# A fourth tile, in SBUF, for the ring of the decays, and the first batch's gate projection placed behind its softplus

## What is computed

```
xc, res = split(x @ W_in.T + b_in)
u       = silu(conv(xc) + conv_b)
dlt, Bm, Cm = split(u @ W_x.T)
delta   = softplus(dlt @ W_dt.T + b_dt)
dA      = exp(delta * A);  dBu = delta * Bm * u
carry   = dA * carry + dBu;  y = sum_n(carry * Cm)
y       = (y * silu(res)) @ W_out.T + b_out
```

## Time and profile before

| | |
|---|---|
| time, median of 3 runs | 2794.74 us (2792.72 to 2795.35) |
| the profiled execution's own time | 2792.28 us |
| its span | 2790.5 us |
| busy: TensorE, VectorE, ScalarE, GpSimd | 87%, 77%, 65%, 74% of the span |
| GpSimd, last product of the mixers | ends at 2207.35 us |
| behind it | the last batches' attention, then the experts; GpSimd is idle there |

### The profile page before, as it was taken

How to read it: one execution, slowest core, us unless ns; L and a number is a source line. 1 busy time by engine, 2 the same in 40 slices (tenths; PEclk the granted TensorE clock), 3 DMA queues, 4 the chain that set the end, 5 groups by cost and what they waited for, 6 DMA issues and landing times. The chain is left out here.

```text
span 2790.5 us, 49779 instructions
## 1 busy us (share of the span) xinstructions
PE 2424.6 (87%) x14816; PEld 1660.6 (60%) x14816; DVE 2140.0 (77%) x3586; ACT 1802.9 (65%) x3972; POOL 2074.5 (74%) x968
## 2 busy tenths in 40 slices
PE   3578888888889898889889888898888879999998
PEld 2345666666666666666666666666665545555554
DVE  1778999999999999999999999999999832322332
ACT  1666777877888888777877787878777541211111
POOL 2999999999999999999999999999999500000000
PEclk8788999999999999999999999999998879999999
DMA  3456566666666666666666666666666360343221
GB/s 118 128 133 149 150 165 168 165 158 157 157 169 166 160 158 165 165 162 168 166 169 164 162 164 166 165 173 163 166 172 158 86 180 12 91 126 96 78 79 31
DMA packets 319323, 399.65 MB, mean 143 GB/s; under 512 B 115697, under 2 KB 256241, under 8 KB 314962
## 3 DMA queue, kind: packets, MB, share of 16 engines
q1 hardware_dynamic: 303698, 384.91, 53.5%
q10 hardware_dynamic: 15360, 11.55, 1.5%
HBM read 300.86 MB, written 94.37 MB: 142 GB/s over the span
## 5 line engine op out<-in xcount | busy, mean ns | idle before, releaser
L506 POOL TENSOR_TENSOR arena<-arena 128x1024 f32<-128x1024 f32 x512 | 1208.2, 2363 | 66.6 <-DMA arena<-w_dram 42.3
L582 ACT ACTIVATE dA_ps<-arena,a_neg 128x252 f32<-128x252 f32 x2048 | 868.7, 461 | 330.4 <-DVE dA_ps L787 172.0
L764 DVE TENSOR_TENSOR_SCAN arena<-dA_ps,arena 128x512 f32<-128x512 f32 x672 | 803.6, 1208 | 112.5 <-ACT dA_ps L582 88.0
L516 POOL TENSOR_TENSOR arena<-arena 128x1024 f32<-128x1024 f32 (+1 forms) x416 | 808.1, 1943 | 17.8 <-DVE arena L764 17.2
L764 DVE TENSOR_TENSOR_SCAN dA_ps<-dA_ps,arena 128x512 f32<-128x512 f32 x352 | 416.2, 1205 | 3.9 <-POOL arena L506 3.7
L887 PE MATMUL a_ps<-xT,w_conv 128*128 128x256 f32 x1536 | 369.8, 391 | 0.0
L829 DVE TENSOR_REDUCE mx<-s_ps 128x2 f32<-128x512 f32 x497 | 334.0, 672 | 23.2 <-PE s_ps L887 23.2
L887 PEld LDWEIGHTS a_ps<-xT,w_conv 128*128 128x128 f32 x1536 | 288.4, 194 | 54.1 <-issue 16.5
L887 PE MATMUL y_ps<-arena,sel 128*32 128x256 f32 x4096 | 257.5, 393 | 55.5 <-DVE m_rows L835 27.8
L640 ACT ACTIVATE probs<-st_ps 128x512 f32<-128x512 f32 x493 | 285.3, 579 | 29.7 <-PE st_ps L887 25.5
L887 PE MATMUL s_ps<-k_st,q_st 96*128 96x256 f32 x994 | 260.6, 344 | 43.7 <-DVE mx L829 28.0
(11 more groups left out here) (111 smaller groups left out, 3272.9 us busy)
## 6 DMA issues: line engine op xcount, KB each, us to landing
arena<-delta_dram SPq DMA_DIRECT2D x512, 128.0 KB, 2.8
arena<-w_dram SPq DMA_DIRECT2D x512, 128.0 KB, 3.2
arena<-bc_dram SPq DMA_DIRECT2D x128, 256.0 KB, 4.5
q_st<-q_parts_dram SPq DMA_DIRECT2D x512, 64.0 KB
k_st<-k_parts_dram SPq DMA_DIRECT2D x512, 64.0 KB
w_dram<-u SPq DMA_DIRECT2D x32, 512.0 KB, 2.8
delta_dram<-delta SPq DMA_DIRECT2D x32, 512.0 KB, 3.8
k_parts_dram<-parts SPq DMA_DIRECT2D x32, 512.0 KB, 4.0
```

The source lines that it names most:

```text
L506: pool.tensor_tensor(dBu[:, n % NB], w_r[:, n // RP % 2, t % RP].unsqueeze(1).to_broadcast([P, QS, L]), bc_r[:, b.par, 0], ALU.mult).then_ ...
L516: pool.tensor_tensor(h[:, n % NH, states], h[:, n % NH, states], bc_r[:, b.par, 1, states], ALU.mult).then_inc(s_hC, 1)
L582: last = nc.scalar.activation(dA[n % NDA][:, q, :, 1:], delta_r[:, n // (2 * RP) % 2, t % RP].rearrange("p (c t) -> p c t", t=CH)[:, :, 1: ...
L764: nc.vector.tensor_tensor_scan(dst, decays, dBu[:, n % NB, 2 * half:2 * half + 2].rearrange("p q t -> p (q t)"), 0.0, ALU.mult, ALU.add).t ...
```

## The change

It has two parts.

**The ring.** `NDA` becomes 4. The fourth member is an SBUF tile `dA_sb` of the same shape; the other three stay in PSUM. Half tile n uses member n modulo 4.

**The start.** SyncE loads the bias parts first, then the convolution's weights and x, then `w_x`, `w_dt` and `w_gate` under a semaphore of their own with no wait between them, then waits for `N_SET` and loads the other seven. VectorE forms the scaled bias rows first; the copy into `bias` becomes a ScalarE instruction; then the convolution's weights. For the first batch alone the four gate projections, their copies and the gate's silu move from the convolutions to behind the softplus (with a table load more). The x projection of the first batch waits for the three front weights, the first state sum for the other seven.

```
-NDA = 3
+NDA = 4
...
-        dA = [bank(f"dA_ps{i}", [P, 2, NCH, CH]) for i in range(NDA)]
+        dA = [bank(f"dA_ps{i}", [P, 2, NCH, CH]) for i in range(NDA - 1)]
+        dA.append(sb("dA_sb", [P, 2, NCH, CH]))
...
+        front_weights = [(w_x[:], "w_x"), (w_dt[:], "w_dt"), (w_gate[:], "w_gate")]
         weights = [
-            (w_gate[:], "w_gate"), (w_x[:], "w_x"), (w_dt[:], "w_dt"), (sel[:], "sel"), (w_out[:], "w_out"),
+            (sel[:], "sel"), (w_out[:], "w_out"),
...
+            for tile, name in bias_parts:
+                sp.dma_start(tile, io[name]).then_inc(s_bias_ld, 16)
             sp.dma_start(w_xc.rearrange("p q t -> p (q t)"), io["w_xc"]).then_inc(s_conv_ld, 16)
             sp.dma_start(conv_rows, io["conv_rows"].partition_broadcast(P)).then_inc(s_conv_ld, 16)
-            for tile, name in bias_parts:
-                sp.dma_start(tile, io[name]).then_inc(s_bias_ld, 16)
             def load_weights():
+                for tile, name in front_weights:
+                    sp.dma_start(tile, io[name]).then_inc(s_front, 16)
+                sp.wait_ge(s_const_v, N_SET)
                 for tile, name in weights:
                     sp.dma_start(tile, io[name]).then_inc(s_const, 16)
-                    sp.wait_ge(s_const_v, N_SET)
                 sp.wait_ge(s_const_p, 4)
...
             act.wait_ge(s_bias_ld, 16 * len(bias_parts))
+            act.wait_ge(s_const_v, N_ROWS)
+            nc.scalar.activation(bias[:], rows, ACT.Copy).then_inc(s_const_a, 1)
             nc.scalar.activation(a_neg[:], a_neg[:], ACT.Exp).then_inc(s_const_a, 1)
...
             def silu(b):
                 act.wait_ge(s_conv, b.value(2, 2))
                 nc.scalar.activation(u[:], u[:], ACT.Silu).then_inc(s_u, 1)
-                act.wait_ge(s_gate, b.value(2, 2))
-                nc.scalar.activation(gate[:, b.par], gate[:, b.par], ACT.Silu).then_inc(s_gsilu, 1)
+                if b.back(1):
+                    silu_gate(b)
                 nc.scalar.preload_act_table_set(EXP_LN)
+            def first_gate(b):
+                if not b.back(1):
+                    for half in range(2):
+                        gate_evac(half)(b)
+                    silu_gate(b)
+                    nc.scalar.preload_act_table_set(EXP_LN)
...
+                (O_SP + 2, first_gate),
...
+            dve.wait_ge(s_bias_ld, 16 * len(bias_parts))
+            nc.vector.tensor_tensor(rows, rows, row_scales, ALU.mult).then_inc(s_const_v, 1)
             dve.wait_ge(s_conv_ld, 32)
...
-            dve.wait_ge(s_bias_ld, 16 * len(bias_parts))
-            nc.vector.tensor_tensor(rows, rows, row_scales, ALU.mult).then_inc(s_const_v, 1)
-            dve.wait_ge(s_const_v, N_CONV - 3)
-            nc.vector.tensor_copy(bias[:], rows).then_inc(s_const_v, 1)
-            dve.wait_ge(s_const_v, N_CONV - 2)
+            dve.wait_ge(s_const_a, 1)
...
-                    if m == 0 and not b.back(1):
-                        pe.wait_ge(s_const, 16 * N_WEIGHTS)
-                        pe.wait_ge(s_const_v, N_SET)
-                        pe.wait_ge(s_const_p, 4)
...
+            def first_gate(b):
+                if not b.back(1):
+                    for m in range(ND):
+                        gate_proj(m)(b)
...
             def x_proj(b):
+                if not b.back(1):
+                    pe.wait_ge(s_front, 16 * len(front_weights))
+                    pe.wait_ge(s_const_v, N_SET)
...
+                    if m == 0 and not b.back(1):
+                        pe.wait_ge(s_const, 16 * N_WEIGHTS)
+                        pe.wait_ge(s_const_p, 4)
...
-                *[(O_GATE + 4 * (m // 2), gate_proj(m)) for m in range(ND)],
+                *[(O_GATE + 4 * (m // 2), later_gate(m)) for m in range(ND)],
+                (O_SP + 1, first_gate),
```

More of the change, by code:

```diff
@@ L279, in mixers @@
         s_const = sem("weights_loaded")
+        s_front = sem("front_weights_loaded")
         s_const_p = sem("const_set_pool")
@@ L329, in mixers @@
         N_WEIGHTS = len(weights)
-        N_CONV = 6 + NDA + TAPS * KD
+        N_ROWS = 3 + NDA
+        N_CONV = 5 + NDA + TAPS * KD
         N_SET = N_CONV + 2
@@ L547, in gate_evac, with silu_gate @@
                 return piece
+            def silu_gate(b):
+                act.wait_ge(s_gate, b.value(2, 2))
+                nc.scalar.activation(gate[:, b.par], gate[:, b.par], ACT.Silu).then_inc(s_gsilu, 1)
             def silu(b):
@@ L551, in silu, with later_gate_evac, piece @@
                 nc.scalar.activation(u[:], u[:], ACT.Silu).then_inc(s_u, 1)
-                act.wait_ge(s_gate, b.value(2, 2))
-                nc.scalar.activation(gate[:, b.par], gate[:, b.par], ACT.Silu).then_inc(s_gsilu, 1)
+                if b.back(1):
+                    silu_gate(b)
                 nc.scalar.preload_act_table_set(EXP_LN)
+            def first_gate(b):
[4 more added lines that the diff above has]
+                    nc.scalar.preload_act_table_set(EXP_LN)
+            def later_gate_evac(half):
+                def piece(b):
+                    if b.back(1):
+                        gate_evac(half)(b)
+                return piece
             def xp_evac(b):
@@ L703, in _ @@
                 (O_SILU, silu),
-                *[(O_GATE + 4 * half + 2, gate_evac(half)) for half in range(2)],
+                *[(O_GATE + 4 * half + 2, later_gate_evac(half)) for half in range(2)],
+                (O_SP + 2, first_gate),
                 (O_K + 1, high(s_k_mm, s_k_hi, s_q_dram, 1)),
@@ L745, in _ @@
             nc.vector.memset(xp[RANK + 2 * NS:RANK + 2 * NS + 1], 1.0).then_inc(s_const_v, 1)
-            dve.wait_ge(s_const_a, 1)
+            dve.wait_ge(s_const_a, 2)
             nc.vector.tensor_scalar(a_neg[:], a_neg[:], -1.0, None, ALU.mult).then_inc(s_const_v, 1)
@@ L918, in gate_proj, with later_gate, piece @@
                 return piece
+            def first_gate(b):
+                if not b.back(1):
+                    for m in range(ND):
+                        gate_proj(m)(b)
+            def later_gate(m):
+                def piece(b):
+                    if b.back(1):
+                        gate_proj(m)(b)
+                return piece
             def x_proj(b):
+                if not b.back(1):
+                    pe.wait_ge(s_front, 16 * len(front_weights))
+                    pe.wait_ge(s_const_v, N_SET)
                 pe.wait_ge(s_u, b.value(1, 1))
```

## The result

The changed kernel took 3040.39 us in the median (3035.71 to 3043.85, 4 runs) against 2795.05 us for the kernel before on the same chip: ratio 1.0876, 95% interval 1.0857 to 1.0895. Forecast were 3150 us. The direction came out as forecast, and so did the lock between the two engines; the size was 245 us instead of 355.

The account below looks back on a forecast made before the run. GpSimd was taken to set the pace, at 64.2 of 66.7 us a batch. 2792.3 + 374 (GpSimd held) - 16 (start) - 0 (fourth bank) = 3150 us; stated range 2765 to 3260, the forecast's own 3060 to 3260.

Parts of the forecast that it names:

- The mechanism: On the SBUF tile, VectorE instructions with two SBUF inputs and GpSimd products reading SBUF block each other; forecast's chance 0.54.
- the 768-column product: At the start, a VectorE product with both inputs in SBUF ran 0.95 us under GpSimd's memset, not held.
- upper end: In each batch, GpSimd is held for 8 scans and 3 products on the SBUF tile: 11.7 us a batch.
- nearer to the copy: Two-SBUF-input cases likened to the start's 2.40 us VectorE copy, which ended 0.41 us behind GpSimd's memset.
- GpSimd stands still for the whole of each: GpSimd loses the full length of 8 scans (1.208 us) and 3 products (0.676) a batch, 374 us in 32 batches.
- 3060: Lower edge of the forecast's own range: the lock lasts three quarters of the VectorE instruction.
- VectorE's waits: Each of 11 VectorE instructions on the tile waits some 1.0 us for GpSimd: 11 us a batch, taken as hidden.
- GpSimd stays the bound: In the batch loop, VectorE at 72.6 us stays below GpSimd's new period of 78.4, so VectorE's waits are hidden.
- rival 3: VectorE becomes the bound: each of 11 instructions waits a whole 2.36 us, 87.6 us a batch, 3445 us; chance 0.08.
- What the fourth place buys: ScalarE runs one half tile further ahead: 0 to 0.7 us a batch, taken as 0.2, then 0 in the sum.
- ScalarE's writes to SBUF: 16 exponentials a batch write SBUF instead of PSUM: 0 to 0.125 us more each, within ScalarE's 13 us of room.
- The start: First batch: convolutions follow each other, gates move behind the softplus; GpSimd's first product near 54.5 instead of 70.65, -16 us.

## Why the prediction was right, and where its sizes were off

- **The mechanism** was right: a VectorE instruction with two SBUF inputs and a GpSimd product shut each other out, in both directions, the second standing still until the first is done. The run with memsets shows it, and shows that the memset beside which the 768-column product ran freely was no proof of the contrary. It also takes away the reason that the prediction gave from the rows for its upper end, that the case is "nearer to the copy": the copy has one input and stood beside a memset, which reads nothing, and beside memsets the scans were free. So that copy is another case than the scans, and by the rows alone the choice was luck.
- **"GpSimd stands still for the whole of each", 11.7 us a batch, 374 us**, is the term that was mis-sized. A GpSimd product that comes second lost 0.92 us to a scan and 0.46 to a product, not 1.21 and 0.68; with all eleven that would be 8.7. That the lock is shorter than the instruction was the prediction's own reason for 3060. The measured time is lower still, because only 126 of the 176 encounters made a product longer, 6.4 us a batch; the others fell into time in which GpSimd waited for VectorE. Its busy time rose by 6.2 us a batch and its waits by 1.9, together the 8.1 of the period. In time: 260 us for the ring, not 374.
- **VectorE's waits**, 11 us a batch, were measured at 12.0. But they were not hidden, as the prediction had it: "GpSimd stays the bound" failed, because GpSimd lost less than was taken. Of VectorE's 11.6 us of added busy time 3.5 went into its idle time, and 8.1 became the period. After the change VectorE is at 98%, GpSimd at 94%, and 68.2 of GpSimd's 68.7 us of waits are for VectorE: these are the signs that the prediction gave for rival 3, with the forecast's wait for each instruction and not with 2.36 us.
- **What the fourth place buys** was taken as 0.2 us a batch, then as nothing. With nothing held it is 1.04 us; I looked at VectorE's 12.1 us of waiting and passed over ScalarE's 85.0 and 48.1 us, behind which other work on the same engine stands.
- **ScalarE's writes to SBUF** cost 492 ns instead of 464, within the bounds: under half a us a batch on an engine that is busy 53.8 of 75.04 us.
- **The start** was taken as 16 us and gave 14.5. The convolution's weights came at 11.10 and not by 10.3, so TensorE began at 16.03 instead of 15.2; the x projection began at 34.73, 15.2 us earlier than before, and at TensorE's slow pace it took 2.67 us instead of 1.97.

## What to carry to other kernels

Before a tile moves from PSUM to SBUF, count the VectorE instructions that would then have two SBUF inputs, and look whether GpSimd reads SBUF beside them: each may wait for the rest of a GpSimd instruction, and GpSimd for it. VectorE, 92% busy with its waits scattered, looked as if it had 5.1 us a batch to give, and 0.74 us more on it came with a longer period. Whether the busiest engine alone sets the pace is told by a run in which its work is cut. For a deeper ring, look also at what stands behind the waits of the in-order engine that fills it.

## What the runs showed of the hardware that was not expected

- A two-input scan held GpSimd for 0.92 us of its own 1.21, a product for 0.46 of 0.68: the exclusion is shorter than the instruction's record.
- Beside GpSimd memsets a scan from SBUF takes 1209 ns, from PSUM 1207: the source costs nothing by itself.
- TensorE's granted clock from 400 to 1600 us went with the pace, 0.98 of 2.4 GHz before, 0.93 after and 0.88 with two banks, while TensorE was busy 89, 84 and 82% of the stretch. For the same matmuls it was busy 59.6 us a batch before and 63.4 after.
